# A graph layer: one row tile of each pair of h turned by a transposing transfer instead of TensorE

## The chip, the cores and the metric

The kernel runs on one core of one Trainium2 chip. The metric is device time in microseconds (us) of one execution; of several executions the median counts. Engines are named as in the profile: PE is TensorE's matmul queue and PEld its weight loads, DVE is VectorE, ACT is ScalarE, POOL is GpSimd, and SP is SyncE, which issues every transfer of this kernel (SPq in the rows).

## The reference

`x` is 8192x256 float32, `adj` 8192x8192 int32 of zeros and ones, the weights are 256x256 (W_comb 512x256).

```python
h = jnp.maximum(_layernorm(x, axis=-1), 0.0)
mask = (adj > 0).astype(x.dtype)
deg = jnp.sum(mask, axis=1, keepdims=True)
agg = mask @ h / jnp.maximum(deg, 1.0)
self_f = h @ W_self + b_self
nb_f = agg @ W_nb + b_nb
combined = jnp.concatenate([self_f, nb_f], axis=-1)
out = jax.nn.relu(combined @ W_comb + b_comb)
x = x + out
```

## The kernel before, in words

The weights are folded first: W_self and W_nb are each multiplied by their half of W_comb (`w12`, 256 rows by 512 columns: 256 for a row's own part, 256 for its part as a neighbour), and all biases make one row (`c_row`). Then there are two stages.

**The projection stage** (the first 110 us) makes `self_f` = h @ w12[own part] and `z` = h @ w12[neighbour part] for 64 tiles of 128 rows, in 32 pairs. Values that TensorE multiplies are held as two fp16 numbers, a high part and the rest (low part), so that three products (TERMS) give nearly float32. Four tiles of x are one chunk (512 KB, 16 chunks, two pairs each). A pair j goes through these steps:

- DVE `stats_of(p)`: mean and variance of the pair's two tiles (L439, L442); the semaphore `aggr_done` counts tiles.
- POOL, once per chunk e, when both pairs have their statistics: four small operations (L253, L255, L257, L260) that make `rstd` and `shift`.
- ACT `norm(j)`: two operations (L269) write h = relu((x - mean) * rstd) over x in `self_f`; `normed` counts them.
- PE `turn(j)`: four 128x128 transposes (L333) into the PSUM buffer `turn_ps`.
- ACT `high_of_h(j)` (L276): turn_ps to fp16, the high part, into `h_t`; DVE `low_of_h(j)` (L447): turn_ps minus the high part, the low part.
- PE `project(j)`: twelve matmuls of 512 columns (L351) into one of RING = 3 buffers `pair_ps`; it waits for `h_low` of its pair and, for the buffer, for `z_low` and `self_copied` of pair j - 3.
- ACT `copy_self(j)` (L285) and `high_of_z(j)` (L280), DVE `low_of_z(j)` (L453) empty the buffer.

Each engine runs its own list in program order, written out by hand, and they meet only at semaphores. PE runs turn(j + 2), project(j). ACT runs in step j: high_of_h(j + 1), norm(j + 3), copy_self(j - 1), high_of_z(j - 1). DVE runs in step j: low_of_h(j + 1), low_of_z(j - 2), stats_of(j + 6), and in the steps 5, 11, 17 and 23 (MASK_STEPS) one quarter of the mask of the first row tile (L424 makes bytes of `stage`, L430 turns them). POOL runs its four operations chunk after chunk and nothing else. SP issues the loads of x and of the first tile's four groups of adj (1 MB each) at the start without a wait, and then each group of the next tiles as its `stage` buffer is free.

**The mask stage** (all the rest) goes over 64 row tiles: for each, 64 matmuls (L360) of the turned mask bytes with z, while DVE and ACT make the mask of the next tile and count its degrees, and DVE finishes a tile with L482, L485 and L488. The buffers `h_t` and `w12` lie in two slots of `mask_t` that the mask stage uses only later; in the rows they are named mask_t, and the statistics lie in x_again.

Of the kernel before, what the change touches and what calls it, by code (L numbers as in the profile page):

```python
# [41 lines left out]
RING = 3  # L42

MASK_STEPS = (5, 11, 17, 23)

# [3 lines left out]
def graph_layer(nc, x, adj, w_self_t, w_nb_t, w_comb, b_cols_in, b_comb, out):  # L49
# [6 lines left out]
    with ExitStack() as ctx:  # L56
# [3 lines left out]
        def sem(name):  # L60
            return ctx.enter_context(nc.semaphore(name))
# [23 lines left out]
        PAIR = 2 * 2 * HALVES * P  # L85
        h_t = spare[:, 0:RING * PAIR].rearrange("p (n i t h m) -> p n i t h m", n=RING, i=2, t=2, h=HALVES)
        w12 = spare[:, RING * PAIR:RING * PAIR + 4 * HALVES * D].rearrange("p (i h n) -> p i h n", i=2, h=HALVES)

# [60 lines left out]
        h_high = sem("h_high")  # L149
        h_low = sem("h_low")  # L150
        projected = sem("projected")
        z_high = sem("z_high")
# [22 lines left out]
        def _(sp):  # L175
# [66 lines left out]
        def _(pool):  # L242
# [7 lines left out]

            for e in range(CHUNKS):
                pool.wait_ge(aggr_done, SUB * (e + 1))
# [6 lines left out]
                pool.wait_ge(negated, e + 1)  # L259
                pool.tensor_tensor(shift[:, e, :], minus_mean[:, e % 2, :], rstd[:, e, :], ALU.mult).then_inc(shift_ready, 1)  # L260

        @block.scalar
        def _(act):
# [8 lines left out]
            def high_of_h(j):  # L272
                act.wait_ge(h_turned, j + 1)
                if j >= RING:
                    act.wait_ge(projected, j - RING + 1)
                act.activation(h_t[:, j % RING, 0, :, :, :].rearrange("p t h m -> p (t h m)"), turn_ps[j % 2][:, :],  # L276
                               ACT.Copy).then_inc(h_high, 1)
# [22 lines left out]
            high_of_h(0)  # L300
            norm(2)

            for j in range(PAIRS + 1):
                if j + 1 < PAIRS:
                    high_of_h(j + 1)
                if j + 3 < PAIRS:
                    norm(j + 3)
                if j >= 1:
                    copy_self(j - 1)
                    high_of_z(j - 1)  # L310
                for a, at in enumerate(COUNT_STEPS):
                    if at == j:
                        count(0, 0, a)
# [11 lines left out]
        def _(pe):  # L325
            def turn(j):
                pe.wait_ge(normed, 2 * (j + 1))
                if j >= 2:
                    pe.wait_ge(h_low, j - 1)
                for t in range(2):  # L330
                    for half in range(HALVES):
                        at = (t * HALVES + half) * P
                        mm = pe.transpose(turn_ps[j % 2][:, at:at + P], self_f[:, 2 * j + t, half * P:(half + 1) * P],  # L333
                                          ident)
                mm.then_inc(h_turned, 1)
# [3 lines left out]
            def project(j):  # L339
                pe.wait_ge(h_low, j + 1)  # L340
                if j == 0:
                    pe.wait_ge(w_ready, 2)
# [5 lines left out]
                for t in range(2):  # L348
                    steps = [(half, i, w) for half in range(HALVES) for i, w in TERMS]
                    for at, (half, i, w) in enumerate(steps):  # L350
                        mm = pe.matmul(pair_ps[j % RING][:, t, :], h_t[:, j % RING, i, t, half, :], w12[:, w, half, :],  # L351
                                       start=(at == 0), stop=(at == len(steps) - 1))
# [65 lines left out]
        def _(dve):  # L418
# [25 lines left out]
            def low_of_h(j):  # L444
                flat = "p t h m -> p (t h m)"
                dve.wait_ge(h_high, j + 1)
                dve.scalar_tensor_tensor(h_t[:, j % RING, 1, :, :, :].rearrange(flat), turn_ps[j % 2][:, :], 1.0,  # L447
                                         h_t[:, j % RING, 0, :, :, :].rearrange(flat), ALU.mult, ALU.subtract
                                         ).then_inc(h_low, 1)

            def low_of_z(j):
# [52 lines left out]
            for m in range(2 * HALVES):  # L504
                dve.tensor_copy(b_wide[:, m, :], b_cols[:, m:m + 1].to_broadcast([P, P])).then_inc(wide_ready, 1)  # L505
            w_low(0)
            w_low(1)
            low_of_h(0)
            for p in range(4, 6):
                stats_of(p)  # L510
            dve.wait_ge(c_product, 1)
            dve.tensor_tensor(c_row[:, :], pair_ps[2][:, 0, 0:D], bc_row, ALU.add).then_inc(c_ready, 1)

            for j in range(PAIRS + 2):
                if j + 1 < PAIRS:
                    low_of_h(j + 1)
                if j >= 2:
                    low_of_z(j - 2)
# [75 lines left out]
```

## Time and profile before

| | us |
|---|---|
| median of three runs (1001.56 to 1003.32) | 1001.75 |
| the profiled execution, its own time | 1001.76 |
| its span (first to last instruction in the profile) | 1000.0 |
| PE busy | 989.9 (99%) |
| DVE busy | 673.9 (67%) |
| ACT busy | 585.0 (59%) |
| POOL busy | 30.5 (3%) |
| granted PE clock | full speed in every slice |

Busy time of PE is modelled from overlapping instructions, so a matmul's duration in the rows is longer than the distance to the next one; the chain in order of time gives the distances. A negative or missing gap between two rows of one engine is such an overlap: the next one starts before the last has ended.

### The profile page before, as it was taken

The page shows a single profiled execution, that of the slowest core. Times are in us where ns is not written, and L with a number is a line of the kernel's source. Part 1 is how long each engine was busy: PE and PEld are TensorE (multiplying, and loading weights), DVE is VectorE, ACT ScalarE, POOL GpSimd, SP SyncE. Part 2 cuts the span into 40 slices and gives each one's busy share as a digit, 9 for nine tenths or more (in the row PEclk, how much of TensorE's full clock was granted, in tenths as well). Part 3 has the DMA queues.
Part 4 walks back from the last instruction along what each step waited for, and adds up shares of the span by engine and source line. Part 5 has one row for each costly group of instructions (what it writes and reads, how often), then busy time and mean ns, then how long its engine had stood idle before and what let it go on. Part 6 is the DMA issues. An engine that isn't in the chain of part 4 may idle for free.

```text
span 1000.0 us, 14269 instructions
## 1 busy us (share of the span) xinstructions
PE 989.9 (99%) x4696; PEld 460.5 (46%) x4696; DVE 673.9 (67%) x1163; ACT 585.0 (59%) x675; POOL 30.5 (3%) x73
## 2 busy tenths in 40 slices
PE   7999999999999999999999999999999999999998
PEld 4555444444444444444444444444444444444443
DVE  6886677986776666766667666676666766667711
ACT  5888886775655556655556555565555655556500
POOL 2332000000000000000000000000000000000000
PEclk9999999999999999999999999999999999999999
DMA  9621399999888898888988888888888888888600
GB/s 344 251 85 43 140 421 371 416 420 377 320 316 321 312 341 317 319 322 312 342 312 322 322 313 336 318 322 322 312 328 328 323 315 321 321 326 326 218 16 10
DMA packets 58994, 295.04 MB, mean 295 GB/s; under 512 B 6624, under 2 KB 24160, under 8 KB 26208
## 3 DMA queue, kind: packets, MB, share of 16 engines
q1 hardware_dynamic: 58976, 294.81, 78.6%
q8 instruction: 10, 0.16, 0.1%
q14 instruction: 8, 0.07, 0.0%
HBM read 286.39 MB, written 8.39 MB: 295 GB/s over the span
## 4 chain that ended last, share of the span: by engine, by line
PE 98%; DMA 1%; DVE 0%; SPq 0%; issue 0%
PE pair_ps L360 89%; PE pair_ps L351 8%; PE turn_ps L333 1%; DMA self_f<-in_x_dram 1%; PE pair_ps L381 0%; DVE x_again L439 0%; SPq L195 0%; SPq L193 0%; DVE z L505 0%; DVE fold L502 0%; DVE x_again L442 0%; DVE part L485 0%; DVE part L482 0%; DVE x_again L488 0%; SPq L177 0%
## 5 line engine op out<-in xcount | busy, mean ns | idle before, releaser
L360 PE MATMUL pair_ps<-z,mask_t 128*128 128x512 f16 x4096 | 885.8, 379 | 0.0
L290 ACT ACTIVATE mask<-mask 128x2048 uint8<-128x2048 uint8 x256 | 488.0, 1908 | 341.4 <-DVE mask_t L430 341.4
L360 PEld LDWEIGHTS pair_ps<-z,mask_t 128*128 128x128 fp8e4 x4096 | 396.2, 98 | 475.7
L430 DVE STREAM_TRANSPOSE mask_t<-mask 128x512 uint32<-128x512 uint32 x256 | 181.7, 710 | 219.8 <-PE pair_ps L360 214.3
L424 DVE TENSOR_SCALAR mask<-stage 128x2048 uint8<-128x2048 int32 x256 | 308.1, 1203 | 6.0 <-DMA stage<-in_adj_dram 5.9
L351 PE MATMUL pair_ps<-mask_t 128*128 128x512 f16 x384 | 87.8, 379 | 0.0
L351 PEld LDWEIGHTS pair_ps<-mask_t 128*128 128x128 f16 x384 | 37.6, 98 | 38.6
L290 ACT ACTIVATION_READ_ACCUMULATOR mask<-mask 128x1 f32 x256 | 48.1, 188 | 0.0
L482 DVE SCALAR_TENSOR_TENSOR part<-pair_ps,rdeg,self_f 128x256 f32<-128x256 f32 x64 | 31.0, 484 | 15.7 <-DVE rdeg L477 11.9
L269 ACT ACTIVATE self_f<-self_f,x_again 128x256 f32<-128x256 f32 x64 | 35.0, 605 | 8.7 <-POOL x_again L260 8.7
L447 DVE SCALAR_TENSOR_TENSOR mask_t<-turn_ps,mask_t 128x512 f16<-128x512 f32 x32 | 21.8, 681 | 19.3 <-ACT mask_t L276 19.3
L485 DVE SCALAR_TENSOR_TENSOR part<-pair_ps,rdeg,part 128x256 f32<-128x256 f32 x64 | 31.0, 484 | 2.3
L488 DVE SCALAR_TENSOR_TENSOR x_again<-part,x_again 128x256 f32<-128x256 f32 x64 | 27.2, 425 | 2.2
L439 DVE BATCH_NORM_STATS2 x_again<-self_f 128x6 f32<-128x256 f32 x64 | 23.7, 411 | 7.3 <-DMA self_f<-in_x_dram 7.3
L285 ACT ACTIVATE self_f<-pair_ps 128x512 f32<-128x512 f32 x32 | 19.1, 597 | 14.8 <-PE pair_ps L351 14.8
L453 DVE SCALAR_TENSOR_TENSOR z<-pair_ps,z 128x512 f16<-128x512 f32 x32 | 21.8, 681 | 5.6 <-ACT z L280 5.6
L470 DVE TENSOR_TENSOR self_f<-self_f,c_row 128x256 f32 (+1 forms) x64 | 24.5, 383 | 0.0
L276 ACT ACTIVATE mask_t<-turn_ps 128x512 f16<-128x512 f32 x32 | 19.3, 603 | 0.0
L461 DVE SCALAR_TENSOR_TENSOR spread<-deg_part,fold 128x128 f16<-128x128 f32 x64 | 18.0, 281 | 1.8 <-ACT mask L290 1.8
L333 PE MATMUL turn_ps<-x_again,self_f 128*128 128x128 f32 x128 | 19.1, 273 | 0.0
L280 ACT ACTIVATE z<-pair_ps 128x512 f16<-128x512 f32 x32 | 19.0, 594 | 0.0
L333 PEld LDWEIGHTS turn_ps<-x_again,self_f 128*128 128x128 f32 x128 | 15.9, 141 | 6.0 <-ACT self_f L269 0.3
(31 smaller groups left out, 93.0 us busy)
## 6 DMA issues: line engine op xcount, KB each, us to landing
stage<-in_adj_dram SPq DMA_DIRECT2D x256, 1024.0 KB, 5.9
self_f<-in_x_dram SPq DMA_DIRECT2D x16, 512.0 KB, 15.4
x_again<-in_x_dram SPq DMA_DIRECT2D x64, 128.0 KB, 5.3
out_dram<-x_again SPq DMA_DIRECT2D x64, 128.0 KB, 5.1
z<-in_L_gnn_W_comb_dram SPq DMA_DIRECT2D x2, 256.0 KB, 4.8
z<-in_L_gnn_W_self_dram SPq DMA_DIRECT2D x1, 256.0 KB, 3.6
z<-in_L_gnn_W_nb_dram SPq DMA_DIRECT2D x1, 256.0 KB, 4.5
z<-in_L_gnn_b_comb_dram SPq DMA_DIRECT2D x1, 128.0 KB, 6.4
```

The costliest lines, as they stand in the source:

```text
L269: act.activation(t, t, ACT.Relu, bias=shift[:, e, s:s + 1], scale=rstd[:, e, s:s + 1]).then_inc(normed, 1)
L290: act.activation(mask[:, a, :], mask[:, a, :], ACT.Copy, accum_out=deg_part[:, n, a:a + 1]).then_inc(counted, 1)
L333: mm = pe.transpose(turn_ps[j % 2][:, at:at + P], self_f[:, 2 * j + t, half * P:(half + 1) * P], ident)
L351: mm = pe.matmul(pair_ps[j % RING][:, t, :], h_t[:, j % RING, i, t, half, :], w12[:, w, half, :], start=(at == 0), stop=(at == len(steps) ...
L360: mm = pe.matmul(acc[n], bytes_of[:, :, s], z16[:, SUB * e + s, :], start=(e == 0 and s == 0), stop=(e == CHUNKS - 1 and s == SUB - 1))
L424: dve.tensor_scalar(mask[:, a, :], stage[:, a, :], 0.0, float(ONE_BYTE), ALU.is_gt, ALU.mult).then_inc(masked, 1)
L430: dve.transpose(mask_t[:, n, :, a, :], src).then_inc(transposed, 1)
L439: dve.bn_stats(stats[:, e % 2, s, :], self_f[:, SUB * e + s, :]).then_inc(stats_done, 1)
L470: dve.tensor_tensor(own_of(r), own_of(r), c_row[:, :], ALU.add).then_inc(biased, 1)
L482: dve.scalar_tensor_tensor(part[:, :], acc[n][:, D:2 * D], rdeg[:, n:n + 1], own, ALU.mult, ALU.add).then_inc(low_added, 1)
L485: dve.scalar_tensor_tensor(part[:, :], acc[n][:, 0:D], rdeg[:, n:n + 1], part[:, :], ALU.mult, ALU.add).then_inc(sum_read, 1)
L488: dve.scalar_tensor_tensor(x_again[:, n, :], part[:, :], 0.0, x_again[:, n, :], ALU.max, ALU.add).then_inc(out_ready, 1)
```

## The change

The second tile of each pair no longer goes through PE. POOL casts its h to fp16 (`cast`), DVE takes the rest against float32 (`rest_of_h`), and one transposing transfer, issued by SP (`move`), turns both halves, 128x512 fp16, into `h_t`, whose layout has the tile ahead of the high and low part. PE's turn, ACT's high_of_h and DVE's low_of_h work on the first tile alone. h_t has PLACES = 4 places instead of 3, and the halves lie in HALVED = 3 places (`h16`). `project(j)` also waits for the transfer's semaphore `h_moved`, and `cast(j)` for that of transfer j - 3, which read its place. POOL's four operations of a chunk are now `rstd_of(e)` and stand between the casts. ACT's norm runs one pair further ahead. SP issues x chunks from the sixth on, and the four groups of adj of the first tile, between the moves; the second tile's groups come after the last move. The diff, cut to its core:

```diff
+PLACES = 4
+HALVED = 3
+
+LOAD_STEPS = (1, 7, 13, 19)
 MASK_STEPS = (5, 11, 17, 23)
...
+            def move(j):
+                at = j % PLACES
+                sp.wait_ge(h_rest, j + 1)
+                if j >= PLACES:
+                    sp.wait_ge(projected, j - PLACES + 1)
+                    sp.wait_ge(h_moved[at], (j // PLACES) * DONE)
+                sp.dma_start_transpose(h_t[:, at, 1, :, :, :].rearrange("p i h m -> p (i h) m"),
+                                       h16[:, j % HALVED, :, :].rearrange("p i d -> p (i d)")
+                                       ).then_inc(h_moved[at], DONE)
...
-            for e in range(2, 6):
+            for e in range(2, 5):
                 load_x(e)
-            for a in range(QUAD):
-                load_group(0, a)
-                load_x(6 + a)
-            for e in range(6 + QUAD, CHUNKS):
-                load_x(e)
+            for j in range(PAIRS):
+                e = j // 2 + 5
+                if j % 2 == 0 and e < CHUNKS:
+                    load_x(e)
+                if j in LOAD_STEPS:
+                    load_group(0, LOAD_STEPS.index(j))
+                move(j)
...
-            for e in range(CHUNKS):
+            def rstd_of(e):
                 pool.wait_ge(aggr_done, SUB * (e + 1))
...
+            def cast(j):
+                pool.wait_ge(normed, 2 * (j + 1))
+                if j >= HALVED:
+                    before = j - HALVED
+                    pool.wait_ge(h_moved[before % PLACES], (before // PLACES + 1) * DONE)
+                pool.tensor_copy(h16[:, j % HALVED, 0, :], self_f[:, 2 * j + 1, :]).then_inc(h_cast, 1)
+
+            rstd_of(0)
+            rstd_of(1)
+            for j in range(PAIRS):
+                cast(j)
+                if j == 0:
+                    rstd_of(2)
+                if j >= 4 and j % 2 == 0 and j // 2 + 1 < CHUNKS:
+                    rstd_of(j // 2 + 1)
...
             high_of_h(0)
             norm(2)
+            norm(3)
 
             for j in range(PAIRS + 1):
                 if j + 1 < PAIRS:
                     high_of_h(j + 1)
-                if j + 3 < PAIRS:
-                    norm(j + 3)
+                if j + 4 < PAIRS:
+                    norm(j + 4)
...
-                for t in range(2):
-                    for half in range(HALVES):
-                        at = (t * HALVES + half) * P
-                        mm = pe.transpose(turn_ps[j % 2][:, at:at + P], self_f[:, 2 * j + t, half * P:(half + 1) * P],
-                                          ident)
+                for half in range(HALVES):
+                    mm = pe.transpose(turn_ps[j % 2][:, half * P:(half + 1) * P],
+                                      self_f[:, 2 * j, half * P:(half + 1) * P], ident)
                 mm.then_inc(h_turned, 1)
...
                 pe.wait_ge(h_low, j + 1)
+                pe.wait_ge(h_moved[j % PLACES], (j // PLACES + 1) * DONE)
...
+            def rest_of_h(j):
+                dve.wait_ge(h_cast, j + 1)
+                dve.scalar_tensor_tensor(h16[:, j % HALVED, 1, :], self_f[:, 2 * j + 1, :], 1.0,
+                                         h16[:, j % HALVED, 0, :], ALU.mult, ALU.subtract).then_inc(h_rest, 1)
...
             w_low(0)
+            rest_of_h(0)
             w_low(1)
             low_of_h(0)
             for p in range(4, 6):
                 stats_of(p)
+            rest_of_h(1)
+            rest_of_h(2)
             dve.wait_ge(c_product, 1)
...
             for j in range(PAIRS + 2):
                 if j + 1 < PAIRS:
                     low_of_h(j + 1)
+                if j + 3 < PAIRS:
+                    rest_of_h(j + 3)
                 if j >= 2:
                     low_of_z(j - 2)
```

How the lists of two engines change. Names: rows are line, operation, out<-in and shape, with the semaphores waited for; x2 is two equal rows. POOL before, the operations of the first chunk and the beginning of the second, whose wait for `aggr_done` is the only one on another engine:

```order
L253 TENSOR_SCALAR x_again<-x_again 128x4 [waits aggr_done]
L255 TENSOR_SCALAR x_again<-x_again 128x4
L257 TENSOR_TENSOR x_again<-x_again 128x4 [waits var_ready]
L260 TENSOR_TENSOR x_again<-x_again 128x4 [waits negated,rstd_ready]
L253 TENSOR_SCALAR x_again<-x_again 128x4 [waits aggr_done]
```

POOL after, in the steady part, from cast(6) through rstd_of(4) and the casts of pairs 7 and 8 to rstd_of(5) (mask_t in these rows is h16, L289 the cast, L275 to L282 the four operations of a chunk):

```order
L289 CAST mask_t<-self_f 128x256 [waits h_moved3,normed]
L275 TENSOR_SCALAR x_again<-x_again 128x4 [waits aggr_done]
L277 TENSOR_SCALAR x_again<-x_again 128x4
L279 TENSOR_TENSOR x_again<-x_again 128x4 [waits var_ready]
L282 TENSOR_TENSOR x_again<-x_again 128x4 [waits negated,rstd_ready]
L289 CAST mask_t<-self_f 128x256 [waits h_moved0,normed]
L289 CAST mask_t<-self_f 128x256 [waits h_moved1,normed]
L275 TENSOR_SCALAR x_again<-x_again 128x4 [waits aggr_done]
```

The four operations of chunk 4, which need the statistics of pairs 8 and 9, now stand between cast(6) and cast(7); before, nothing stood behind them but the next chunk's.

DVE before, from stats_of(9), the last of step 3, to the end of low_of_z(2) in step 4:

```order
L439 BN_STATS x_again<-self_f 128x6 x2
L442 BN_AGGR x_again<-x_again 128x2 [waits stats_done]
L442 BN_AGGR x_again<-x_again 128x2
L447 SCALAR_TENSOR_TENSOR mask_t<-turn_ps,mask_t 128x512 [waits h_high]
L453 SCALAR_TENSOR_TENSOR z<-pair_ps,z 128x2x256 [waits z_high]
```

DVE after, the same place (L485 is low_of_h(5), L491 rest_of_h(7), L496 low_of_z(2)):

```order
L477 BN_STATS x_again<-self_f 128x6 x2
L480 BN_AGGR x_again<-x_again 128x2 [waits stats_done]
L480 BN_AGGR x_again<-x_again 128x2
L485 SCALAR_TENSOR_TENSOR mask_t<-turn_ps,mask_t 128x256 [waits h_high]
L491 SCALAR_TENSOR_TENSOR mask_t<-self_f,mask_t 128x256 [waits h_cast]
L496 SCALAR_TENSOR_TENSOR z<-pair_ps,z 128x2x256 [waits z_high]
```

Between low_of_h and low_of_z DVE now has one instruction more, and it waits for `h_cast`, which POOL raises.

## Rows read from the trace of the kernel before

**Rows 1.** The page, part 4: the chain that ended last, by line.

```profile
PE pair_ps L360 89%; PE pair_ps L351 8%; PE turn_ps L333 1%; DMA self_f<-in_x_dram 1%; PE pair_ps L381 0%; DVE x_again L439 0%; SPq L195 0%; SPq L193 0%; DVE z L505 0%; DVE fold L502 0%; DVE x_again L442 0%; DVE part L485 0%; DVE part L482 
```

**Rows 2.** The chain in order of time: start us, us, what.

```profile
18.15 2.59 PE pair_ps L351 x12
...
60.08 0.44 PE turn_ps L333 x4
60.52 2.59 PE pair_ps L351 x12
...
110.66 37.99 PE pair_ps L360 x176
```

**Rows 3.** Timeline of DVE, one pair: start us, us, engine, line, operation, [idle before].

```profile
59.91 0.74 DVE L439 BATCH_NORM_STATS2 x_again<-self_f 128x6 f32<-128x256 f32 x2
60.68 0.25 DVE L442 BATCH_NORM_AGGREGATE x_again<-x_again 128x2 f32<-128x6 f32 x2
61.73 0.69 DVE L447 SCALAR_TENSOR_TENSOR mask_t<-turn_ps,mask_t 128x512 f16<-128x512 f32 x1 [0.80 <-ACT mask_t L276]
62.34 0.68 DVE L453 SCALAR_TENSOR_TENSOR z<-pair_ps,z 128x512 f16<-128x512 f32 x1
```

**Rows 4.** Timeline of ACT, the wait that it has once per pair.

```profile
63.15 0.60 ACT L285 ACTIVATE self_f<-pair_ps 128x512 f32<-128x512 f32 x1 [0.48 <-PE pair_ps L351]
```

**Rows 5.** Timeline of POOL: a start-up operation, then one chunk's first and last.

```profile
1.38 0.29 POOL L248 TENSOR_SCALAR_AFFINE_SELECT x_again<-x_again 128x128 f32<-128x128 f32 x1 [0.24 <-POOL eight L246]
...
61.02 0.19 POOL L253 TENSOR_SCALAR x_again<-x_again 128x4 f32<-128x4 f32 x1 [4.24 <-DVE x_again L442]
...
62.61 0.20 POOL L260 TENSOR_TENSOR x_again<-x_again 128x4 f32<-128x4 f32 x1
```

**Rows 6.** Groups by line, 0 to 165 us: busy us, mean ns of one | idle.

```profile
L447 DVE SCALAR_TENSOR_TENSOR mask_t<-turn_ps,mask_t 128x512 f16<-128x512 f32 x32 | 21.8, 681 | 19.3 <-ACT mask_t L276 19.3
...
L430 DVE STREAM_TRANSPOSE mask_t<-mask 128x512 uint32<-128x512 uint32 x23 | 16.4, 711 | 0.9
...
L257 POOL TENSOR_TENSOR x_again<-x_again 128x4 f32<-128x4 f32 x16 | 16.6, 1037 | 0.0
...
L461 DVE SCALAR_TENSOR_TENSOR spread<-deg_part,fold 128x128 f16<-128x128 f32 x5 | 1.4, 282 | 0.0
...
L488 DVE SCALAR_TENSOR_TENSOR x_again<-part,x_again 128x256 f32<-128x256 f32 x2 | 0.8, 424 | 0.1
```

**Rows 7.** Timeline of DVE and of POOL where a mask is formed.

```profile
30.58 1.19 DVE L424 TENSOR_SCALAR mask<-stage 128x2048 uint8<-128x2048 int32 x1
...
30.75 1.07 POOL L253 TENSOR_SCALAR x_again<-x_again 128x4 f32<-128x4 f32 x1 [3.53 <-DVE x_again L442]
```

**Rows 8.** Timeline of DVE, then of POOL, ahead of project(1).

```profile
12.46 1.28 DVE L493 SCALAR_TENSOR_TENSOR mask_t<-pair_ps,mask_t 128x512 f16<-128x512 f32 x2
...
14.26 0.74 DVE L439 BATCH_NORM_STATS2 x_again<-self_f 128x6 f32<-128x256 f32 x2
...
15.96 0.25 DVE L442 BATCH_NORM_AGGREGATE x_again<-x_again 128x2 f32<-128x6 f32 x2
...
12.93 0.20 POOL L260 TENSOR_TENSOR x_again<-x_again 128x4 f32<-128x4 f32 x1
```

**Rows 9.** The page, part 6: transfers, KB each, median us from issue to landing.

```profile
x_again<-in_x_dram SPq DMA_DIRECT2D x64, 128.0 KB, 5.3
out_dram<-x_again SPq DMA_DIRECT2D x64, 128.0 KB, 5.1
...
z<-in_L_gnn_W_self_dram SPq DMA_DIRECT2D x1, 256.0 KB, 3.6
```

**Rows 10.** Windows: engines' busy us (count), PE clock, DMA share, GB/s.

```profile
10.00:20.00 10.00, 9.59 (x53) 6.25 (x52) 9.23 (x37) 6.60 (x14) 3.56 (x10) 1.00 1.03 424
40.00:50.00 10.00, 10.00 (x54) 5.34 (x53) 7.73 (x20) 8.55 (x19) 2.70 (x5) 1.00 0.03 11
```

More of the change, by code:

```diff
@@ L85, in graph_layer @@
         PAIR = 2 * 2 * HALVES * P
-        h_t = spare[:, 0:RING * PAIR].rearrange("p (n i t h m) -> p n i t h m", n=RING, i=2, t=2, h=HALVES)
-        w12 = spare[:, RING * PAIR:RING * PAIR + 4 * HALVES * D].rearrange("p (i h n) -> p i h n", i=2, h=HALVES)
+        W_AT = PLACES * PAIR
+        H_AT = W_AT + 4 * HALVES * D
+        h_t = spare[:, 0:W_AT].rearrange("p (n t i h m) -> p n t i h m", n=PLACES, t=2, i=2, h=HALVES)
+        w12 = spare[:, W_AT:H_AT].rearrange("p (i h n) -> p i h n", i=2, h=HALVES)
+        h16 = spare[:, H_AT:H_AT + HALVED * 2 * D].rearrange("p (n i d) -> p n i d", n=HALVED, i=2)
         late = z16[:, 3 * TILES // 4:, :].rearrange("p t n -> p (t n)").bitcast(F32)
@@ L150, in graph_layer @@
         h_low = sem("h_low")
+        h_cast = sem("h_cast")
+        h_rest = sem("h_rest")
+        h_moved = [sem(f"h_moved{n}") for n in range(PLACES)]
         projected = sem("projected")
@@ L273, in high_of_h @@
                 act.wait_ge(h_turned, j + 1)
-                if j >= RING:
-                    act.wait_ge(projected, j - RING + 1)
-                act.activation(h_t[:, j % RING, 0, :, :, :].rearrange("p t h m -> p (t h m)"), turn_ps[j % 2][:, :],
+                if j >= PLACES:
+                    act.wait_ge(projected, j - PLACES + 1)
+                act.activation(h_t[:, j % PLACES, 0, 0, :, :].rearrange("p h m -> p (h m)"), turn_ps[j % 2][:, 0:D],
                                ACT.Copy).then_inc(h_high, 1)
@@ L350, in project @@
                     for at, (half, i, w) in enumerate(steps):
-                        mm = pe.matmul(pair_ps[j % RING][:, t, :], h_t[:, j % RING, i, t, half, :], w12[:, w, half, :],
+                        mm = pe.matmul(pair_ps[j % RING][:, t, :], h_t[:, j % PLACES, t, i, half, :], w12[:, w, half, :],
                                        start=(at == 0), stop=(at == len(steps) - 1))
@@ L444, in low_of_h @@
             def low_of_h(j):
-                flat = "p t h m -> p (t h m)"
+                flat = "p h m -> p (h m)"
                 dve.wait_ge(h_high, j + 1)
-                dve.scalar_tensor_tensor(h_t[:, j % RING, 1, :, :, :].rearrange(flat), turn_ps[j % 2][:, :], 1.0,
-                                         h_t[:, j % RING, 0, :, :, :].rearrange(flat), ALU.mult, ALU.subtract
+                dve.scalar_tensor_tensor(h_t[:, j % PLACES, 0, 1, :, :].rearrange(flat), turn_ps[j % 2][:, 0:D], 1.0,
+                                         h_t[:, j % PLACES, 0, 0, :, :].rearrange(flat), ALU.mult, ALU.subtract
                                          ).then_inc(h_low, 1)
+            def rest_of_h(j):
+                dve.wait_ge(h_cast, j + 1)
+                dve.scalar_tensor_tensor(h16[:, j % HALVED, 1, :], self_f[:, 2 * j + 1, :], 1.0,
+                                         h16[:, j % HALVED, 0, :], ALU.mult, ALU.subtract).then_inc(h_rest, 1)
             def low_of_z(j):
```

## The prediction

> **What bounds the kernel now.** I read the page first: its chain of waits puts 89% of the span on TensorE's (PE's) line 360, the mask tiles, and 8% on its line 351, the projection [rows 1]. The chain in order of time shows what one pair costs: four transposes of h in 0.44 us, twelve matmuls in 2.59 us, and so on without a gap, from 18.15 us (project(1)) to the start of the first mask tile at 110.66 us [rows 2]. So in this stage a pair takes 3.03 us, and after it the 64 tiles run back to back, 64 matmuls and 13.8 us each (37.99 / 176 x 64 [rows 2]). What the change does can only show in these first 110 us, and all that counts is when the first mask tile starts. Then the timelines of the other engines, for how much room they have under 3.03 us. VectorE (DVE) works 2.22 us per pair and waits 0.80 us for ScalarE (ACT) [rows 3]. ACT waits 0.48 us per pair for the projection, so it works 2.55 us [rows 4]. GpSimd (POOL) runs four small operations per chunk of two pairs and idles over 4 us between; nobody waits for it, since it starts when the statistics of a chunk are ready and ACT needs the result much later [rows 5].
>
> **TensorE.** Two of four transposes go: 0.44 / 2 = 0.22 us per pair [rows 2]. If TensorE stays the bound, a pair takes 2.81 us. ACT's copy of h loses 256 of 512 elements; by VectorE's rows (681 ns for 512, 282 ns for a 128-element operation of the same kind [rows 6], 1.04 ns per element) I take 0.27 us off low_of_h and 0.21 off ACT's copy, which leaves ACT at 2.34 us, below 2.81: no term.
>
> **VectorE.** It loses 0.27 us and gains rest_of_h, 128x256 from SBUF: 424 ns by the nearest row [rows 6], 0.35 us of spacing since neighbours overlap by 0.08 (L447 is 0.69 long, the next starts after 0.61 [rows 3]). 2.22 - 0.27 + 0.35 = 2.30 us per pair, also below 2.81. Busy time alone says that this fits.
>
> **The wait that is added.** The order excerpts say something else. rest_of_h(j+3) stands second in VectorE's step j and waits for cast(j+3) on POOL. POOL has rstd_of(j/2+1) between cast(j) and cast(j+1), for even j from 4. And rstd_of(e) waits for the statistics of chunk e, which VectorE finishes with the last instruction of the step just before the one in which it wants that cast. For instance: stats_of(9) ends step 3; only then can POOL run the four operations of rstd_of(4), then cast(7); and in step 4, after low_of_h(5), VectorE stands at rest_of_h(7) until it is there. low_of_z and the next statistics queue behind it, and project(j+1) waits for low_of_z(j-2), since it reuses that PSUM buffer. The slack that POOL's work had is gone, once per two pairs.
>
> The round of two steps, from one end of statistics to the next: POOL's four operations 1.88 us (60.93 to 62.81 us [rows 3, 5]), cast c, 0.06 to VectorE, rest 0.35, low_of_z 0.60, statistics 1.02 (59.91 to 60.93), then the second step: low_of_h 0.34, rest 0.35, low_of_z 0.60, statistics 1.02. With c = 0.50 that is **6.72 us per two pairs**, against 6.05 now and 5.62 if TensorE bound. The second cast of a round isn't late: its norms end 1.1 us after POOL's four, the cast 0.5 later, and VectorE comes to it 2.9 us after them.
>
> c isn't in the trace. The nearest row reads and writes 128 elements in 0.29, half as many [rows 5]: 0.29 is the lower end, 0.58 that row doubled, and as part of 0.29 is fixed I take 0.50. The upper end is POOL's longest plain operation, the power of L257, 1.04 [rows 6].
>
> Four rounds are longer. While VectorE forms a mask (L424), POOL's first operation takes 1.07 instead of 0.19 us, so its four end 2.76 after the statistics instead of 1.88 [rows 5, 7]. The masks of steps 5, 11, 17 and 23 all come right after the second half of a chunk, where POOL starts. The mask work itself (1.20 + 0.71 us [rows 6, 7]) then lies beside POOL's and is the shorter. So 6.72 + 0.88 = 7.6 us. The Trainium skill (SBUF — State Buffer, Who interferes with whom) says that such a VectorE operation and a GpSimd one exclude each other entirely; the trace agrees, 1.07 against 0.19 us.
>
> Waits of this kind come at the even steps 2 to 26, which makes twelve rounds: 8 x 6.72 + 4 x 7.6 = 84.2 us.
>
> **The start.** cast(0) follows POOL's second four, which end at 13.13 [rows 8]: 13.63. rest_of_h(0) 13.69 to 14.04, the second w_low to 14.64, low_of_h(0) to 14.98, statistics of pairs 4 and 5 (1.95 us from 14.26 to 16.21 now [rows 8]) to 16.93. POOL has rstd_of(2) ahead of cast(1): 16.93 + 1.88 = 18.81, cast(1) 19.31, rest_of_h(1) done 19.80. Its transfer: no row shows a transposing one. On an empty queue 256 KB of weights land 3.6 us after issue, 128 KB stores and loads after 5.1 and 5.3 among other traffic [rows 9]; the bytes alone, at 424 GB/s [rows 10], would be 0.3. I take 3.5, ends 0.3 and 5.3. It lands at 23.35, and project(1) starts then instead of 18.15: **+5.2 us**. On: cast(4) waits for the same landing, 23.85; rest_of_h(4) to 24.26, statistics 25.28, POOL 27.16, cast(5) 27.66, rest_of_h(5) at 27.72. That is the first of the twelve rounds.
>
> **Sum.** rest_of_h(29) starts at 27.72 + 84.2 = 111.9, low_of_z(24) ends 1.04 later (0.35 + 0.69), project(27) starts at 113.0. From there TensorE is the bound: 2 x 2.81 + 3 x 2.59 = 13.4, end 126.4 against 110.66 now: **+15.7 us**. Of these 5.2 are the start, 10.9 the 26 pairs between (89.65 against 78.7), -0.4 the end. Span 1000.0 + 15.7, and 1.76 around it as in the profiled execution (1001.76, equal to the median of 1001.75): 1017.5 us.
>
> **Terms at nothing.** Transfers in the stage: rest_of_h(j) comes three steps before cast(j+3) needs its landing, some 10 us, so a landing of 5.3 is hidden, also with 1 MB of adj ahead (2.5 us at 424 GB/s); the DMA engines stand at 3% of their time at 40 to 50 us [rows 10]. On SP's queue, x chunks and the four adj loads of tile 0 are now issued between moves, but seven steps and more before VectorE wants them. The four loads of tile 1, issued at steps 5 to 24 until now, stand behind move(31), at step 28; they take 10 us, and VectorE wants them after step 33. Tile 1's mask then has 13.8 us of the first tile as cover, as now.
>
> **Rivals.** *The waits hide, TensorE bounds.* 26 pairs lose 0.22 each (-5.7), the end 0.4, the start adds 5.2: 1001.76 - 0.9 = 1000.9; with landings of 0.3 us the start adds only 3.1 (turn(3) waits for low_of_h(1), at 20.95), and it is 998.8. This is the case that isn't slower. It decides at a round of 5.62 us: the chain from statistics to cast would have to be 1.1 us shorter. For it: each engine's busy time fits. Against it: POOL's 1.88 us rest on an operation that takes 1.04 in each of its 16 turns [rows 6]. *Transfers are slow.* If they can't overlap and each takes the 5.3 us of a 128 KB row, they set the pace: 19.85 + 31 x 5.3 + 2.59 = 186.7 at the end of projection, +76, 1078 us. It decides above 3.4 us per transfer. For it: four blocks through one mechanism whose rate no row shows. Against it: 128 KB rows take that long from latency and company, while 1 MB passes in 2.5 us. The Trainium skill has a page for each side: VectorE: DVE Perf Modes (The three transpose paths) gives 1309 ns for 128x128, which for four one after another would be an estimated 5.2 us and this rival; Advanced Engine Details and Errata (X-Bar Transpose) has transposing transfers as fast as others, and then nothing is added. No run here shows either yet. *The transfer is hidden anyway and the order is harmless too, but the transposes don't free TensorE's time*: 3.03 us per pair stay, 1001.76 + 5.2 = 1007; slower, below my range.
>
> **Chances.** Forecast mechanism 0.84, TensorE-bound 0.07, slow transfers 0.06, no TensorE time freed 0.03. Range of the forecast: c enters sixteen times (twelve rounds, casts 0, 1, 4 and 5), so -3.4 and +8.6; the landing once, -2.1 and +1.8: 1012.0 to 1027.9, given as 1012 to 1028. 0.2% (2 us) is about what can be told from no change here: faster 0.04 and the same 0.05 come from the TensorE-bound case with a little room, the rest is slower, 0.91.
>
> **What would show it.** VectorE idle at rest_of_h until POOL's cast, 2.1 us at each even step from 2 to 26 and 1.1 behind a mask; PE idle at project until low_of_z; two pairs per 6.7 us, per 7.6 around masks; project(1) near 23; the first mask tile near 126; from there 13.8 us per tile as now. POOL's four at 1.88 us, right after the statistics. Wrong if PE runs gapless at 2.81 us per pair, if PE or the casts wait for DMA past project(1), or if cast is far from 0.5 us.

## The result and the profile after

The changed kernel takes **1014.98 us** (median of 4 runs, 1014.38 to 1015.71), the kernel before 1001.69 (4 runs, 1001.56 to 1003.32): ratio 1.0129 (95%: 1.0115 to 1.0144), so slower by about 13.3 us. Predicted: 1017.5 (1012 to 1028), slower with 0.91. The profiled execution took 1015.71 us, its span is 1013.9.

The page, parts 4, 5 and 6 (against [rows 1, 6, 9]):

```profile
PE 89%; DVE 3%; issue 3%; ACT 2%; POOL 1%; DMA 1%; SPq 0%; POOLq 0%; ACTq 0%
...
L389 PE MATMUL pair_ps<-mask_t 128*128 128x512 f16 x384 | 89.4, 384 | 13.4 <-ACT self_f L323 11.2
...
L307 ACT ACTIVATE self_f<-self_f,x_again 128x256 f32<-128x256 f32 x64 | 34.6, 595 | 39.4 <-POOL x_again L282 39.4
...
L491 DVE SCALAR_TENSOR_TENSOR mask_t<-self_f,mask_t 128x256 f16<-128x256 f32 x32 | 13.7, 431 | 23.4 <-POOL mask_t L289 23.4
...
mask_t<-mask_t SPq DMA_TRANSPOSE x32, 3.0
```

L389 is the projection (L351 before), L307 ScalarE's norm, L491 rest_of_h. TensorE no longer carries the front of the kernel: VectorE, ACT and POOL have entered the chain. The time is lost where it was expected, before the first mask tile. From there to the end it is 889.3 us, as before. The chain in order of time, one round of two pairs, one round with a mask, and the end of the stage (against [rows 2]):

```profile
51.39 0.67 DVE x_again L477 x2
...
55.24 0.57 ACT self_f L323
...
56.60 0.42 DVE mask_t L485
...
57.96 0.67 DVE x_again L477 x2
58.99 1.07 POOL x_again L275
...
65.41 0.67 DVE x_again L477 x2
...
111.06 2.75 PE pair_ps L389 x12
...
124.60 1.51 PE pair_ps L398 x7
```

A plain round takes 57.96 - 51.39 = 6.57 us, one with a mask 65.41 - 57.96 = 7.45; project(27) starts at 111.06 and the first mask tile at 124.60, against 110.66. The waits of the first 135 us (engine line <- what it waited for: us in total, times, longest):

```profile
POOL x_again L275 <- DVE x_again L480: 52.3, 16, 4.5
ACT self_f L307 <- POOL x_again L282: 39.4, 15, 6.0
DVE mask_t L491 <- POOL mask_t L289: 23.4, 16, 2.2
...
PE pair_ps L389 <- ACT self_f L323: 11.2, 11, 1.7
...
POOL mask_t L289 <- DMA mask_t<-mask_t: 2.3, 1, 2.3
...
PE pair_ps L389 <- DMA mask_t<-mask_t: 0.8, 1, 0.8
```

The transposing transfers cost one wait of 2.3 us and one of 0.8, both at the start. The forecast wait is the third row. The second row is not in the forecast: ACT too waits for POOL's four (L282 is the last of them). The fourth names ACT's copy_self (L323) for PE's wait and not low_of_z; below it turns out that this name is wrong. The timeline of that round (start us, us, engine, line, operation, [idle before <- releaser]):

```profile
50.86 0.59 ACT L323 ACTIVATE self_f<-pair_ps 128x512 f32<-128x512 f32 x1
...
54.01 0.20 POOL L282 TENSOR_TENSOR x_again<-x_again 128x4 f32<-128x4 f32 x1
54.15 0.40 POOL L289 CAST mask_t<-self_f 128x256 f16<-128x256 f32 x1
54.24 1.09 ACT L307 ACTIVATE self_f<-self_f,x_again 128x256 f32<-128x256 f32 x2 [2.02 <-POOL x_again L282]
...
54.58 0.43 DVE L491 SCALAR_TENSOR_TENSOR mask_t<-self_f,mask_t 128x256 f16<-128x256 f32 x1 [1.90 <-POOL mask_t L289]
...
54.92 0.68 DVE L496 SCALAR_TENSOR_TENSOR z<-pair_ps,z 128x512 f16<-128x512 f32 x1
...
55.24 0.57 ACT L323 ACTIVATE self_f<-pair_ps 128x512 f32<-128x512 f32 x1
...
55.86 2.75 PE L389 MATMUL pair_ps<-mask_t 128*128 128x512 f16 x12 [0.80 <-ACT self_f L323]
...
56.19 0.38 ACT L314 ACTIVATE mask_t<-turn_ps 128x256 f16<-128x256 f32 x1
...
56.30 0.25 DVE L480 BATCH_NORM_AGGREGATE x_again<-x_again 128x2 f32<-128x6 f32 x2
```

**Two paths** leave POOL's four at 54.21. This is step 10 of the lists: the projection at 55.86 is eight rounds, 16 pairs, ahead of project(27), so it is project(11). VectorE's path: cast(13), rest_of_h(13) at 54.58, low_of_z(8) 0.34 us behind it, to 55.60, and then project(11), which needs that low_of_z. ACT's path: norm(14), which stands one pair further ahead than cast(13), at 54.24; behind it copy_self(9), 55.24 to 55.81, high_of_z(9) (L318) and high_of_h(12) (L314), which ends at 56.57. VectorE's next low_of_h (L485, 56.60) waits for that; its own statistics ended at 56.55. It is ACT's path that the chain shows.

**What PE waits for.** project(11) needs copy_self(8), and that was done at 51.45 (the first row). The copy that ends at 55.81, which the profile names, is copy_self(9), and only project(12) needs it. The releaser in brackets is inferred from the last update of a semaphore, and the count that was waited for is not looked at. So PE waits for low_of_z here, as the forecast says; in c_act below, where the profile names low_of_z itself, PE starts the same 0.26 us behind its end (53.28 to 53.54).

### The profile page after: what moved, and what is told of

It is laid out like the page before. It is cut to its first block, busy times and chain, and to the rows that moved or that the text cites. A ratio compares the mean times of both kernels' runs of the same rounds, so it can differ in the third digit from the quotient of the medians.

```text
span 1013.9 us, 14323 instructions
## 1 busy us (share of the span) xinstructions
PE 987.9 (97%) x4632; PEld 453.9 (45%) x4632; DVE 677.6 (67%) x1195; ACT 576.9 (57%) x675; POOL 42.4 (4%) x105
## 4 chain that ended last, share of the span: by engine, by line
PE 89%; DVE 3%; issue 3%; ACT 2%; POOL 1%; DMA 1%; SPq 0%; POOLq 0%; ACTq 0%
PE pair_ps L398 87%; PE pair_ps L389 1%; DVE x_again L477 1%; DVE z L496 1%; ACT self_f L323 1%; PE pair_ps L412 1%; POOL x_again L275 1%; DMA z<-in_L_gnn_W_comb_dram 1%; ACT z L318 1%; DVE mask_t L485 1%; DVE mask_t L491 0%; ACT self_f L307 0%; DVE x_again L480 0%; ACT mask_t L314 0%; POOL x_again L277 0%
## 5 line engine op out<-in xcount | busy, mean ns | idle before, releaser
L389 PE MATMUL pair_ps<-mask_t 128*128 128x512 f16 x384 | 89.4, 384 | 13.4 <-ACT self_f L323 11.2
L389 PEld LDWEIGHTS pair_ps<-mask_t 128*128 128x128 f16 x384 | 37.1, 99 | 55.7 <-issue 18.1
L307 ACT ACTIVATE self_f<-self_f,x_again 128x256 f32<-128x256 f32 x64 | 34.6, 595 | 39.4 <-POOL x_again L282 39.4
L491 DVE SCALAR_TENSOR_TENSOR mask_t<-self_f,mask_t 128x256 f16<-128x256 f32 x32 | 13.7, 431 | 23.4 <-POOL mask_t L289 23.4
L496 DVE SCALAR_TENSOR_TENSOR z<-pair_ps,z 128x512 f16<-128x512 f32 x32 | 21.9, 684 | 5.9 <-ACT z L318 5.9
L323 ACT ACTIVATE self_f<-pair_ps 128x512 f32<-128x512 f32 x32 | 18.7, 585 | 3.1 <-PE pair_ps L389 3.1
L318 ACT ACTIVATE z<-pair_ps 128x512 f16<-128x512 f32 x32 | 19.0, 592 | 0.0
L518 DVE TENSOR_SCALAR deg<-pair_ps 128x1 f32<-128x1 f32 x32 | 3.9, 122 | 20.4 <-PE pair_ps L404 20.4
L279 POOL TENSOR_TENSOR x_again<-x_again 128x4 f32<-128x4 f32 x16 | 16.6, 1037 | 0.0
L518 DVE TENSOR_SCALAR deg<-turn_ps 128x1 f32<-128x1 f32 x32 | 4.0, 125 | 18.6 <-PE turn_ps L404 15.3
```

The lines of the kernel that those rows point to most:

```text
L307: act.activation(t, t, ACT.Relu, bias=shift[:, e, s:s + 1], scale=rstd[:, e, s:s + 1]).then_inc(normed, 1)
L318: act.activation(z16[:, 2 * j:2 * j + 2, 0:D], pair_ps[j % RING][:, :, D:2 * D], ACT.Copy, scale=Z_SCALE).then_inc(z_high, 1)
L323: act.activation(self_f[:, 2 * j:2 * j + 2, :], pair_ps[j % RING][:, :, 0:D], ACT.Copy, scale=SELF_SCALE).then_inc(self_copied, 1)
L389: mm = pe.matmul(pair_ps[j % RING][:, t, :], h_t[:, j % PLACES, t, i, half, :], w12[:, w, half, :], start=(at == 0), stop=(at == len(steps ...
L496: dve.scalar_tensor_tensor(z16[:, 2 * j:2 * j + 2, D:2 * D], pair_ps[j % RING][:, :, D:2 * D], Z_SCALE, z16[:, 2 * j:2 * j + 2, 0:D], ALU. ...
```

## The experiments

My theory after the result, in two parts: (1) POOL's four operations, released by stats_of(j+6) at the end of a step, are needed at once by both VectorE (through the cast) and ACT (through the norm), and the two paths have nearly the same length; (2) the start adds the rest. Rivals: TensorE or the transfers bound; the removed transposes save nothing; one path alone does it. All kernels are edits of the changed one. The kernel before had 1002.12, 1002.42 and 1002.13 us as medians on the same chips, against 1001.69 beside the changed kernel, so a difference to the changed kernel's 1014.98 can be off by up to 0.7 us from this alone.

**a_stats: the statistics one pair earlier.**

```diff
-                if j + 6 < PAIRS:
-                    stats_of(j + 6)
+                if j == 0:
+                    stats_of(6)
+                if j + 7 < PAIRS:
+                    stats_of(j + 7)
```

> The changed kernel with VectorE's statistics one pair further ahead (stats_of(j + 7) in step j, stats_of(6) in step 0). Theory 1 (statistics, POOL's four operations and what waits for them make the round of 6.6 us): POOL's four then end a step before VectorE's rest_of_h and ScalarE's norm want them, both waits vanish, TensorE bounds at 2.81 us per pair; the start stays, so 1001 us, up to 1003 with the 1.7 us of the halved clock in project(1). Rival (the transfers, or SP's queue, hold the casts): no change, 1015 us.

Measured: **1001.32 us** (10 runs, 1000.79 to 1002.34), ratio to before 0.9995 (0.9985 to 1.0004): no difference that can be told. Against the changed kernel that is 13.7 us back from moving one pair's statistics, 1 us of work, by one step. Its waits, 0 to 115 us, and its chain in order of time:

```profile
ACT self_f L307 <- POOL x_again L282: 12.7, 5, 6.1
```

```profile
21.92 4.33 PE pair_ps L389 x12
26.57 2.59 PE pair_ps L389 x12
...
110.17 17.91 PE pair_ps L398 x83
```

From 26.57 on the pairs are 2.81 us apart without a gap, just what 3.03 less two transposes gives. So TensorE's 0.22 us per pair is real and comes to count as soon as it bounds. The start stays late (project(1) at 21.92 against 18.15 [rows 2]), project(1) itself is long (4.33 us, see the clock at the end), and together they eat what 26 pairs gain.

**b_pool: POOL does the cast before its four operations.** This takes VectorE's path away and leaves ACT's.

```diff
-                if j >= 4 and j % 2 == 0 and j // 2 + 1 < CHUNKS:
+                if j >= 5 and j % 2 == 1 and j // 2 + 1 < CHUNKS:
```

> The changed kernel with POOL's rstd_of(j/2 + 1) one cast later, behind cast(j + 1), so that rest_of_h(j + 1) no longer stands behind it; statistics and ScalarE's order stay. Theory A (the prediction's: VectorE's wait at rest_of_h sets the round): VectorE no longer waits there, 1001 to 1004 us. Theory B (ScalarE's norm(j + 4), one pair further ahead than before, waits for the same four operations, and copy_self behind it holds the PSUM buffer): the round via ScalarE is 1.88 + 1.00 for two norms + 0.48 + 0.47 + 0.38 + 0.34 + 0.33 + 0.60 + 1.03, which is 6.5 us, so the time stays within 1 us of 1015.

Measured: **1017.77 us** (4 runs, 1017.23 to 1019.31), 1.0157 (1.0140 to 1.0174) of before: 2.8 us more than the changed kernel. Its waits:

```profile
ACT self_f L307 <- POOL x_again L282: 42.9, 15, 6.0
...
DVE mask_t L485 <- ACT mask_t L314: 25.7, 13, 3.2
```

rest_of_h no longer waits for a cast in the rounds, and nothing is gained. VectorE's idle time has moved to low_of_h, which waits for ACT's high_of_h (L314); the plain rounds are 6.74 us in the chain. The wait that I had forecast as the cause could be removed whole without a gain, and without ACT's path I could not have explained this. That it even costs was not expected (within 1 us of 1015): 0.17 us per plain round is POOL's second operation (L277), which has a median of 0.40 us there against 0.23 in the changed kernel; the rest of the 2.8 is left open.

**c_act: ACT's norm last in its step.** This leaves VectorE's path alone.

```diff
-                if j + 4 < PAIRS:
-                    norm(j + 4)
...
+                if j + 4 < PAIRS:
+                    norm(j + 4)
```

> The changed kernel with ScalarE's norm(j + 4) last in its step, behind copy_self and high_of_z, so that its wait for POOL no longer holds the PSUM buffer; POOL's and VectorE's order stay. Theory (two paths through POOL's four operations, each of 6.5 us per round, the one over rest_of_h and the one over norm): the path over VectorE is untouched and holds the time, 1013 to 1015.5 us. Rival (only the path over ScalarE binds, as TensorE's wait for copy_self suggests): 1001 to 1004 us.

Measured: **1012.66 us** (4 runs, 1012.02 to 1013.20), 1.0105 (1.0089 to 1.0120) of before, 2.3 us below the changed kernel. Its waits:

```profile
DVE mask_t L491 <- POOL mask_t L289: 23.8, 16, 2.2
...
PE pair_ps L389 <- DVE z L496: 10.3, 11, 1.5
```

ACT's copies now come earlier in the step, and the profile names low_of_z for PE's wait. rest_of_h starts at 48.13, 54.53 and 61.81 in its chain, rounds of 6.40 and 7.28 us. So the forecast path alone takes 6.40 us per round, ACT's alone 6.74 in b_pool's order, and the two together 6.57 in the changed kernel. The time is 0.3 us below the expected 1013 to 1015.5.

**bc_both: b_pool and c_act together.**

> The changed kernel with both: rstd_of behind cast(j + 1) on POOL, and norm last in ScalarE's step. Theory of the two paths: neither wait is in a round any more; what is left (POOL's four 1.88, two norms 1.00, high_of_h 0.38, low_of_h 0.34, rest_of_h 0.33, low_of_z 0.60, statistics 1.03, with hand-overs some 5.7) is at TensorE's 5.62: 1001 to 1004 us. Rival (a third thing, the casts behind the norms, or the transfers, takes over): over 1008 us.

Measured: **1005.05 us** (8 runs, 1004.69 to 1005.39), 1.0027 (1.0016 to 1.0037) of before. Apart the two edits give +2.8 and -2.3 us, together -9.9. PE's timeline between two masks:

```profile
51.56 2.75 PE L389 MATMUL pair_ps<-mask_t 128*128 128x512 f16 x12
54.15 0.38 PE L370 MATMUL turn_ps<-x_again,self_f 128*128 128x128 f32 x2
54.36 2.75 PE L389 MATMUL pair_ps<-mask_t 128*128 128x512 f16 x12
57.36 0.41 PE L370 MATMUL turn_ps<-x_again,self_f 128*128 128x128 f32 x2 [0.24 <-DVE mask_t L485]
```

Gapless at 2.80 until a mask comes. That is two parallel paths: one removed shows little, both removed give back most of the loss. 1001 to 1004 was expected. What is left, 3.7 us over a_stats, are the stalls at the four masks: from 54.36 to 58.40 it is 4.04 us and not 2.81.

**t_turn4: the two removed transposes put back on TensorE, their results unused.**

```diff
+                for half in range(HALVES):
+                    mm = pe.transpose(turn_ps[j % 2][:, D + half * P:D + (half + 1) * P],
+                                      self_f[:, 2 * j + 1, half * P:(half + 1) * P], ident)
```

> The changed kernel with the two removed transposes of each pair put back on TensorE, into the unused half of turn_ps, read by nobody (extra work, nothing left out). Theory (TensorE isn't the bound of the projection stage now): 0.22 us more per pair fit into TensorE's idle time of the rounds, only the last six or so pairs and the start pay, at most +1.5 us, 1015 to 1016.5. Rival (TensorE still bounds): +6.6 us, 1021.6.

Measured: **1015.01 us** (4 runs, 1014.80 to 1016.26), 1.0130 (1.0113 to 1.0147) of before, the same as the changed kernel and as expected. 32 x 0.22 = 7 us of TensorE's work disappears in its waits: TensorE doesn't bound this stage.

**f_start: casts 0 and 1 on POOL right behind the first rstd_of, and rest_of_h(0) and (1) earlier on VectorE.** POOL then runs rstd_of(1) behind these two casts and rstd_of(2) behind cast(2).

```diff
+            cast(0)
+            cast(1)
...
-            for j in range(PAIRS):
+            for j in range(2, PAIRS):
...
-                if j == 0:
+                if j == 2:
...
+                if p == 1:
+                    rest_of_h(0)
...
-            rest_of_h(0)
+            rest_of_h(1)
...
-            rest_of_h(1)
```

> The changed kernel with the casts of pairs 0 and 1 right behind rstd_of(0) on POOL and rest_of_h(0) and (1) correspondingly earlier on VectorE; steady part as it is. Theory (the start costs 5.2 us because cast(1) stands behind rstd_of(2)): project(1) starts near 18.5 instead of 23.4 and TensorE has no idle stretch that halves its clock: 4 to 6 us less, 1009 to 1011. Rival (the first transfers land late because of the queue of x behind which they stand): project(0) and (1) still wait for a transfer, under 2 us gained, 1013 to 1014.

Measured: **1013.24 us** (4 runs, 1012.77 to 1013.50), 1.0110 (1.0093 to 1.0127) of before. PE's timeline, in the changed kernel and then in f_start:

```profile
18.18 2.75 PE L389 MATMUL pair_ps<-mask_t 128*128 128x512 f16 x12 [1.39 <-issue]
22.14 0.41 PE L370 MATMUL turn_ps<-x_again,self_f 128*128 128x128 f32 x2 [1.21 <-DVE mask_t L485]
23.37 4.44 PE L389 MATMUL pair_ps<-mask_t 128*128 128x512 f16 x12 [0.82 <-DMA mask_t<-mask_t]
```

```profile
19.83 2.75 PE L391 MATMUL pair_ps<-mask_t 128*128 128x512 f16 x12
```

project(1) starts 3.5 us earlier and the first mask tile at 121.50, 3.1 earlier in the trace, but 1.7 us by the medians, less than the 4 to 6 expected. Part of the 3.5 belongs to the one execution that was profiled of the changed kernel: a_stats, whose lists are the same up to there, has project(1) at 21.92. The start adds its own few us, ahead of the rounds.

**af_both: a_stats and f_start together.**

> Statistics one pair further ahead and the early casts of pairs 0 and 1 together. Theory: a_stats (1001.3 us) less the start's gain (project(1) 3 us earlier, by f_start's trace against the changed kernel's) and less the 1.7 us of project(1) at the halved clock, since TensorE no longer idles ahead of it: 996 to 998.5 us. Rival (something else holds the first pairs once TensorE bounds): 999 to 1001 us.

Measured: **998.06 us** (5 runs, 997.65 to 998.47), 0.9957 (0.9944 to 0.9971) of before, 4.4 us below its 1002.42 and within the expected range. The first mask tile starts at 106.79 (110.66 before). project(0) starts at 17.36, since the first transfer, issued beside adj loads, took 7.2 us to land.

**x_double and x_four: every transfer issued twice, on top of a_stats.** The extra copies go to places that nobody reads, and the casts wait for them too; in x_double they go to one place, so that SP waits for the last extra before it issues the next, in x_four to four in turn. The edit of x_four, cut:

```diff
+                if j >= PLACES:
+                    sp.wait_ge(h_extra[at], (j // PLACES) * DONE)
+                sp.dma_start_transpose(extra[at], h16[:, j % HALVED, :, :].rearrange("p i d -> p (i d)")
+                                       ).then_inc(h_extra[at], DONE)
```

> a_stats with every transposing transfer issued twice, the first time into an unused place, and the casts waiting for both (extra work, nothing left out). Theory (transfers are hidden in the steady part with landings of 3.0 us and some 7 us of room): only the first pairs pay, by one transfer's issue of 1.19 us on SP's queue or two, 1001.3 to 1005 us. Rival (transfers are near their limit: 2.81 us per pair against two issues of 1.19 and two transfers of some 1 us at the engines): several us per ten pairs, over 1010 us.

> As x_double (a_stats with every transposing transfer issued twice, casts waiting for both; extra work, nothing left out), but the extra ones go to four unused places in turn, so that SP waits for the landing of the extra one four pairs back and not of the last one. Theory (x_double's 23 us came from its own wait on SP: 3.1 us from one extra issue to its landing, up to 5.4, is more than the 2.81 us of a pair): with that wait gone two transfers per pair fit, 1001.3 to 1006 us. Rival (the transfers themselves are near a limit of the DMA engines or of SP's issue, 2 x 1.2 us of 2.81): 1015 us or more.

Measured: **1024.33 us** (4 runs, 1024.27 to 1024.83), 1.0219 (1.0204 to 1.0235), and **1011.08 us** (4 runs, 1010.96 to 1012.09), 1.0086 (1.0071 to 1.0102). Both are above what was expected (1001.3 to 1005, and to 1006). The difference of 13 us is the wait that I had built into x_double myself, so only x_four speaks on the transfers. One of its windows (engines' busy us, PE clock, DMA share, GB/s):

```profile
60.00:80.00 20.00, 18.97 (x96) 9.55 (x95) 16.65 (x47) 15.59 (x35) 7.48 (x18) 1.00 1.06 218
```

With twice the transfers the 16 DMA engines are full, at 218 GB/s and not at the 424 of the plain loads [rows 10]; of the 4.35 MB in this window 2.6 MB are plain loads, so the transposing transfers alone are slower still. In the changed kernel itself:

```profile
40.00:50.00 10.00, 8.56 (x43) 4.12 (x42) 6.95 (x22) 6.88 (x16) 4.08 (x10) 1.00 0.51 135
...
84.00:86.00 2.00, 2.00 (x10) 0.88 (x9) 1.91 (x7) 2.00 (x6) 0.00 (x0) 1.00 0.41 66
86.00:88.00 2.00, 2.00 (x12) 1.03 (x10) 1.25 (x5) 0.83 (x3) 0.89 (x3) 1.00 0.32 66
```

Half full, where before they stood at 3% [rows 10]; in these 10 us two chunks of x pass beside three transposing transfers. In 84 to 88 us two such transfers pass and nothing else (66 GB/s x 4 us = 264 KB), for (0.41 + 0.32) x 2 = 1.46 us of all engines: 0.73 us each, or 180 GB/s. My "hidden" holds with one transfer per pair; with two it costs some 10 us over a_stats. Whether the engines or SP's queue is the limit then isn't separated: two issues of 1.19 us and half an x load of 0.57 make 2.67 of a pair's 2.81 us.

**l_front: the second part of the change undone, all x chunks and the four adj groups of tile 0 issued ahead of the first transfer.**

```diff
-            for e in range(2, 5):
+            for e in range(2, 6):
+                load_x(e)
+            for a in range(QUAD):
+                load_group(0, a)
+                load_x(6 + a)
+            for e in range(6 + QUAD, CHUNKS):
...
-                e = j // 2 + 5
-                if j % 2 == 0 and e < CHUNKS:
-                    load_x(e)
-                if j in LOAD_STEPS:
-                    load_group(0, LOAD_STEPS.index(j))
```

> The changed kernel with all chunks of x and the four adj groups of the first tile issued ahead of the first move, as in the kernel before: the second part of the change undone alone. Theory (a transfer stands behind all that SP issued earlier): the loads keep the DMA engines until about 43 us as before, move(0) lands after that, project(0) starts at 44 to 46 instead of 18.2, and while TensorE waits the statistics run ahead only as far as VectorE's order lets them; the same 6.6 us rounds follow: 25 us or so more, 1038 to 1043 us. Rival (a small transfer passes between the packets of the loads): within 3 us of 1015.

Measured: **1035.92 us** (4 runs, 1035.65 to 1036.15), 1.0335 (1.0319 to 1.0351) of before, 20.9 us over the changed kernel; 1038 to 1043 was expected, with the landing after 43 us. One window at its start, the landings of its transfers up to 60 us, and PE's first projection:

```profile
24.00:30.00 6.00, 0.00 (x0) 0.00 (x0) 0.00 (x0) 0.00 (x0) 0.00 (x0) 0.50 1.00 410
```

```profile
DMA to landing us min/median/max: 2.4/2.4/15.4
```

```profile
39.71 5.28 PE L389 MATMUL pair_ps<-mask_t 128*128 128x512 f16 x12 [24.75 <-issue]
```

The first transfer, issued at 24.2 us, landed 15.4 us later behind the loads; no engine computed from 24 to 30 us. Spreading the loads over the steps is what makes the turn by transfer bearable.

**g_best: af_both, with x chunks 4 and 5 behind the first two transfers and the first adj group at step 3 in place of 1.**

> af_both with x chunks 4 and 5 issued behind move(0) and move(1), and the first adj group behind move(2) instead of move(0), so that the first transfer, which took 7.2 us to land beside 1 MB of adj and two chunks of x, has the DMA engines sooner. Theory: project(0) starts near 15.4 instead of 17.4, TensorE is gapless from there: 996 us, between 995.5 and 997. Rival (the packets of what was issued earlier aren't what holds it): 998 us as af_both.

Measured: **997.25 us** (5 runs, 997.13 to 997.46), 0.9949 (0.9936 to 0.9963) of before. PE's timeline:

```profile
18.25 2.75 PE L393 MATMUL pair_ps<-mask_t 128*128 128x512 f16 x12
21.95 0.41 PE L374 MATMUL turn_ps<-x_again,self_f 128*128 128x128 f32 x2 [0.95 <-DVE mask_t L489]
```

project(1) starts 2.1 us earlier than in af_both (20.39), and 0.95 of that goes at once to a wait for low_of_h. This is the best version found: 17.7 us below the changed kernel and 4.9 below the kernel before, 0.25 above the expected 995.5 to 997.

## Why the prediction was right, and where it was not

| step of the prediction | forecast | measured |
|---|---|---|
| time, side | 1017.5, slower | 1014.98, slower |
| rest_of_h waits for the cast behind POOL's four | sixteen casts late, 2.1 us each, 1.1 at a mask | 23.4 us in 16 waits, 1.90 and 0.96 each in the rounds |
| plain round, mask round | 6.72, 7.6 us | 6.57, 7.45 us |
| cast | 0.50 us (0.29 to 1.04) | 0.400 us |
| POOL's first operation under a mask | 1.07 us | 1.07 us |
| project(1) | 23.35 us | 23.37 us |
| landing of the transfer | 3.5 us | 2.4 at least, 3.0 median |
| project(27), first mask tile | 113.0, 126.4 us | 111.06, 124.60 us |
| PE waits for | low_of_z | low_of_z (the profile names copy_self, see above) |
| ACT | "below 2.81: no term" | a path of its own, 6.57 us per round where VectorE's alone has 6.40 |
| TensorE if it bounds | 2.81 us per pair | 2.81 us (a_stats) |

**Right:** that TensorE's saving can't be had because a chain of waits through POOL sets the pace, once per two pairs; a_stats shows it by moving one pair's statistics and getting 13.7 us back, t_turn4 by putting the saving back without a cost.

**The main mis-sized term** is the round. The cast took 0.400 us, not 0.50. In sixteen places that is 1.6 us of the 1.8 by which the first tile was forecast late (126.4 against 124.60). Within VectorE's path the estimate was still longer: c_act has that path alone and rounds of 6.40, where mine with the measured cast would be 6.62. The rest I had in operations whose spacing is shorter than I took it: in c_act the statistics in the middle of a round take 0.94 to the next operation and not 1.02, and the cast starts 1.80 us after the statistics' end and not 1.88; the other 0.06 are spread over the small spacings. That this did not show as a further miss is due to a second error, which adds 0.17 to each plain round.

**The step that failed** is the term of ACT, "below 2.81: no term". I looked at ACT's busy time alone, although I had written a few lines below, of VectorE, that busy time is not enough. ACT's norm runs one pair ahead of the cast, so it needs the same chunk's POOL results just as early, and high_of_h, for which VectorE's next low_of_h waits, stands behind it. "project(j+1) waits for low_of_z(j-2)" held; my recorded expectations for b_pool and c_act, which let ACT's path hold TensorE over the PSUM buffer, took the profile's name for PE's wait at its word. b_pool shows ACT's path alone (1017.77), c_act the other alone (1012.66), bc_both neither (1005.05). The forecast came out well because the two are nearly of one length, and that is luck; a proposal to reorder POOL, which my text would have justified, would have made it slower.

**The start** hit 23.35 by parts that cancel. The second transfer was issued at 20.82 and not at 19.85, and landed 2.42 us later and not 3.5. The 1 us of delay is there already when POOL's second four end, at 14.18 against the 13.13 that I had carried over from the trace of before. They wait for the statistics of pairs 2 and 3, and these began at 10.31 us, when the second chunk of x had landed, against 9.26 in the trace of before. That lies in the single execution: a_stats and t_turn4, whose orders ahead of project(1) are the same but for two extra transposes a pair in t_turn4, have project(1) at 21.92 and 22.22. So the hit at 23.37 is luck.

**The transfers** were hidden as forecast (2.3 us of POOL's waits and 0.8 of PE's, at the start), so the rival of slow transfers fell: 5.3 us each would have given 1078 by its sum. The Trainium skill, VectorE: DVE Perf Modes (The three transpose paths), gives 1309 ns for 128x128; the trace doesn't bear out four of these in a row, as 128x512 lands 2.4 us after its issue and keeps the DMA engines for 0.73. Nor does it bear out the Trainium skill, Advanced Engine Details and Errata (X-Bar Transpose), "TRN2 transpose DMAs are as fast as regular DMAs": the 128 KB from SBUF to SBUF in 0.73 us are 180 GB/s, the plain loads have 424 [rows 10]. The reserve I claimed ("the DMA engines stand at 3%") was real; the transfers used up about a fifth of it (0.73 of some 3.3 us per pair), the x chunks that the change moved into the stage about as much again.

## What to carry to other kernels

When an operation is put between two engines, list for every engine which of its instructions need the same late result, not only the one that the change adds: two waits side by side must both go before either is worth much, and the one that is removed alone may even cost. Busy time per step bounds an engine from below only; the round from a result, through all who queue behind it and back, is the figure to compare. When a profile names what ended a wait, check by the order of the lists that it is the update that was waited for. Where a small producer (here statistics, 1 us) releases such a round, issuing it one step earlier is the cheapest cure, and transfers that a computation waits for must not be queued behind bulk loads.

## What the runs showed of the hardware

**A transposing transfer**, 128x512 in fp16 from SBUF to SBUF, occupies SP's queue for 1.19 us, twice a plain load's 0.57, lands after 2.4 us at the least, and keeps all DMA engines for about 0.73 us (180 GB/s, a plain load has 424). Behind other loads the landing grew to 7.4 us, in l_front to 15.4. In the changed kernel, up to 60 us:

```profile
L207 SPq DMA_TRANSPOSE mask_t<-mask_t x15: 1189/1190/1302, 15.0 to 57.4; - x15
```

**The clock.** project(1) took 4.44 us in the changed kernel and 2.75 in f_start. The windows of the changed kernel:

```profile
21.00:23.00 2.00, 0.41 (x2) 0.20 (x2) 1.98 (x6) 2.00 (x5) 0.05 (x1) 1.00 0.32 66
...
24.00:25.00 1.00, 1.00 (x4) 0.43 (x3) 0.96 (x4) 0.00 (x0) 0.00 (x0) 0.51 0.95 311
...
27.00:28.00 1.00, 1.00 (x6) 0.60 (x5) 0.59 (x2) 0.93 (x2) 0.37 (x2) 0.79 0.69 213
```

TensorE worked only 0.41 of the 2 us from 21 to 23; from 24 to 27 the granted clock is 0.50 to 0.51, the level of 1.2 GHz, and during 27 to 28 it returns to 2.4. In the changed kernel this costs nothing, since its rounds don't pass through project(1). In a_stats, where TensorE bounds, it does: 4.33 us instead of the 2.75 that af_both has there. So a short stall at the start of a TensorE-bound stage can cost its own length and 1.6 us more. It doesn't always: TensorE worked 0.63 of the 2 us from 20 to 22 in t_turn4 and 0.05 of the one from 21 to 22 in g_best, and the clock stayed at 1.00 in both.
